# Down product of the experts in rounded parts, on one Trainium2 core

## What is computed

```python
xb = x[token_buf].reshape(E, CAP, H)
gu = jnp.einsum('ech,ehf->ecf', xb, W_gate_up)
g, u = jnp.split(gu, 2, axis=-1)
inter = jax.nn.silu(g) * u
yb = jnp.einsum('eci,eih->ech', inter, W_down)
yb = yb * w_buf.reshape(E, CAP, 1)
routed = jnp.zeros((T, H), x.dtype).at[token_buf].add(yb.reshape(E * CAP, H))
shared = jax.nn.silu(x @ Wsg) * (x @ Wsu) @ Wsd
```

## Time and profile before

| | |
|---|---|
| median of 3 runs | 711.11 us (708.4 to 711.25) |
| profiled execution | 710.25 us, its span 708.6 us |
| PE busy | 675.0 us, 95% of the span |
| PEld busy | 630.5 us, 89% |
| DVE busy | 471.5 us, 67% |
| ACT busy | 331.9 us, 47% |
| POOL busy | 210.5 us, 30% |
| PE's part of the chain that ended last | 67% |

### The profile page before, as it was taken

How to read it: one execution, slowest core, us unless ns; L and a number is a source line. 1 busy time by engine, 2 the same in 40 slices (tenths; PEclk the granted TensorE clock), 3 DMA queues, 4 the chain that set the end, 5 groups by cost and what they waited for, 6 DMA issues and landing times.

```text
span 708.6 us, 16559 instructions
## 1 busy us (share of the span) xinstructions
PE 675.0 (95%) x4587; PEld 630.5 (89%) x4588; DVE 471.5 (67%) x1486; ACT 331.9 (47%) x803; POOL 210.5 (30%) x312
## 2 busy tenths in 40 slices
PE   6979999999999999999999999999999999999993
PEld 6879988999989888889999999999999999999993
DVE  2357788887888888666576666666666666666651
ACT  1335555645556565444444444444444444444431
POOL 3113223232233300310333333333333324242430
PEclk9989999999999999999999999999999999999998
DMA  8136344544444232621454544445464545454531
GB/s 280 44 101 218 112 131 144 172 131 136 145 136 144 88 104 54 181 71 25 99 110 99 110 99 102 108 99 111 97 113 97 113 97 113 97 113 97 113 56 20
DMA packets 74180, 79.36 MB, mean 112 GB/s; under 512 B 6361, under 2 KB 65897, under 8 KB 74154
## 3 DMA queue, kind: packets, MB, share of 16 engines
q1 hardware_dynamic: 61706, 65.81, 33.1%
q0 software_dynamic: 12160, 12.60, 11.0%
q10 hardware_dynamic: 288, 0.66, 0.3%
HBM read 51.73 MB, written 19.32 MB: 100 GB/s over the span
## 4 chain that ended last, share of the span: by engine, by line
PE 67%; DVE 12%; DMA 8%; issue 7%; ACT 2%; POOL 1%; DVEq 1%; POOLq 0%; ACTq 0%; SPq 0%
PE bank L1220 19%; PE bank L1030 9%; PE bank L1190 9%; PE bank L1239 7%; PE bank L1018 6%; PE bank L1202 6%; DMA result<-y_rows,put_idx 5%; PE bank L1060 3%; PE bank L1240 3%; DMA result<-s_rows 1%; DVE s_inter L1657 1%; DVE stats L1387 1%; PE bank L1088 1%; DVE w_raw L1483 1%; DVE h L1411 1%
## 5 line engine op out<-in xcount | busy, mean ns | idle before, releaser
L1657 DVE TENSOR_TENSOR s_inter<-s_gate,bank 128x384 f32<-128x384 f32 (+1 forms) x112 | 60.3, 539 | 68.7 <-PE bank L1220 58.8
L1239 PE MATMUL bank<-s_dn,s_in_hi 128*128 128x384 f32 (+1 forms) x287 | 87.3, 365 | 3.3 <-DVE s_rows L1672 3.0
L865 ACT ACTIVATE s_gate<-bank 128x384 f32<-128x384 f32 (+1 forms) x112 | 53.5, 479 | 67.7 <-PE bank L1220 67.7
L1030 PE MATMUL bank<-w_tok,patches 128*128 128x192 f32 x384 | 72.7, 343 | 8.2 <-DMA patches<-xp 6.9
L689 POOL DMA_INDIRECT result<-y_rows,put_idx x40 | 65.4, 1635 | 38.1 <-DVE y_rows L1644 15.3
L1220 PE MATMUL bank<-all_hiA,s_hi 128*128 (+4 forms) x210 | 73.5, 350 | 2.0 <-DVE s_inter L1657 0.6
L760 ACT ACTIVATE y<-h,shift,rstd 128x192 f32<-128x192 f32 (+2 forms) x96 | 45.6, 538 | 59.4 <-POOL shift L623 59.4
L1030 PEld LDWEIGHTS bank<-w_tok,patches 128*128 128x128 f32 x384 | 65.7, 200 | 8.1 <-issue 8.1
L1240 PE MATMUL bank<-s_dn,s_in_lo 128*128 128x192 f32 (+1 forms) x287 | 72.0, 251 | 0.0
L1220 PE MATMUL bank<-all_B,s_lo 128*128 (+4 forms) x210 | 70.1, 334 | 0.0
L1220 PE MATMUL bank<-all_B,s_hi 128*128 (+4 forms) x210 | 70.1, 334 | 0.0
(11 more groups left out here) (205 smaller groups left out, 1846.4 us busy)
## 6 DMA issues: line engine op xcount, KB each, us to landing
raw_gu<-wgu SPq DMA_DIRECT2D x22, 464.0 KB, 5.0
raw_gu<-wgu SPq DMA_DIRECT2D x44, 232.0 KB, 5.9
patches<-xp SPq DMA_DIRECT2D x16, 588.0 KB, 4.4
down_w<-wdn SPq DMA_DIRECT2D x22, 348.0 KB
result<-s_rows POOLq DMA_DIRECT2D x13, 288.0 KB
result<-h SPq DMA_DIRECT2D x16, 192.0 KB
yw_rows<-y SPq DMA_DIRECT2D x16, 192.0 KB
all_hiA<-y_hiA SPq DMA_DIRECT2D x16, 162.5 KB, 2.6
```

The lines of the kernel that those rows point to most:

```text
L865: act.activation(s_gate[m % 2][0:r, 0:width], up_banks(m, alone)[0][0:r, 0:width], ACT.Silu).then_inc(s_gate_ready, 1)
L1030: mm = pe.matmul(tok_ps[:, t * D:(t + 1) * D], own[:, c, t * 128:(t + 1) * 128], w_tok[:, c, :], start=c == 0, stop=c == KC - 1)
L1239: pe.matmul(bank[0:r, 0:2 * D], s_in_hi[:, m, rows], s_dn[:, m, :], start=m == 0, stop=False)
L1657: dve.tensor_tensor(s_inter[m % 2][0:r, 0:width], s_gate[m % 2][0:r, 0:width], up, ALU.mult).then_inc(s_inter_ready, 1)
```

## The change

The down product is split as the others are. ACT rounds `down_w` to `down_hi` (`down_part`, 116 x 768 in one instruction) and `inter` to `inter_hi` (`inter_part`, two instructions of 116 x 384 for an expert); DVE makes the rests (`down_low`, `inter_low`). `down` then runs three rounded products where one fp32 product stood, so twelve for a half.

The rests need room. `gu_lo` now lies over `raw_gu`, `down_lo` over `down_w` and `inter_lo` over `inter`: each rest is written over the data it is taken from. So the next gate and up weights may be loaded only when the products with `gu_lo` have run, and SP's wait goes from `gu_split` to `gu_mm`. PE's `down` waits for `down_split` and `inter_split` where it waited for the load and for `inter_ready`.

```diff
+        inter_at = chunks.at
...
+        raw_gu_at = experts.at
         raw_gu = [sb(f"raw_gu{p}", [128, 2, 2 * I]) for p in range(2)]
+        down_at = experts.at
         down_w = [sb(f"down_w{p}", [F, EM, D]) for p in range(2)]
...
-        gu_lo = [sb(f"gu_lo{p}", [128, 2, 2 * I], F32R) for p in range(2)]
+        down_hi = [sb(f"down_hi{p}", [F, EM, D], F32R) for p in range(2)]
+        inter_hi = sb("inter_hi", [F, EM, CAP], F32R)
+        over_raw = Region(raw_gu_at).place
+        gu_lo = [over_raw(f"gu_lo{p}", [128, 2, 2 * I], F32R) for p in range(2)]
+        over_down = Region(down_at).place
+        down_lo = [over_down(f"down_lo{p}", [F, EM, D], F32R) for p in range(2)]
+        inter_lo = Region(inter_at).place("inter_lo", [F, EM, CAP], F32R)
...
-                        wait_apart(sp, passed, (gu_split, 4 * j + 2 * n - 2))
+                        wait_apart(sp, passed, (gu_mm, 8 * j + 4 * n - 4))
...
+                def down_part(j, n):
+                    act.wait_ge(down_in[n % 2], arrivals(j, n, n % 2, 16))
+                    act.activation(down_hi[n % 2][:, :, :], down_w[n % 2][:, :, :], ACT.Copy).then_inc(down_hi_ready, 1)
+
+                def inter_part(j, n, i):
+                    act.wait_ge(inter_ready, 8 * j + 4 * n + 2 * i + 2)
+                    own = slice(2 * i, 2 * i + 2)
+                    act.activation(inter_hi[:, own, :], inter[:, own, :], ACT.Copy).then_inc(inter_hi_ready, 1)
...
                 gu_part(0, 0, 1)
+                down_part(0, 0)
...
                     s_hi_part(o, WIDTH, 0)
                     silu(j, 0, 2)
                     s_silu(o, WIDTH, 2)
+                    inter_part(j, 0, 0)
                     s_hi_part(o, WIDTH, 1)
                     gu_part(j, 1, 1)
                     silu(j, 0, 3)
                     s_silu(o, WIDTH, 3)
+                    inter_part(j, 0, 1)
                     s_hi_part(o, WIDTH, 2)
                     split_x(j, 1)
                     s_silu(o, WIDTH, 4)
                     s_hi_part(o, WIDTH, 3)
+                    down_part(j, 1)
                     silu(j, 1, 0)
                     s_hi_part(o, WIDTH, 4)
                     s_silu(o, WIDTH, 5)
...
                     s_hi_part(o, WIDTH, 5)
                     silu(j, 1, 2)
                     s_silu(o, WIDTH, 7)
+                    inter_part(j, 1, 0)
                     s_hi_part(o, WIDTH, 6)
                     s_hi_part(o, WIDTH, 7)
                     silu(j, 1, 3)
                     s_half(o, PER_PAIR * j + ADDED_AHEAD, WIDTH, TILES, 0)
                     split_x(j, 2)
+                    inter_part(j, 1, 1)
                     gu_part(j, 2, 1)
+                    down_part(j, 2)
                     s_half(o, 0, WIDTH, TILES, 1)
                     s_half(o, 0, WIDTH, TILES, 2)
 
...
                         pe.wait_ge(y_ready, 2 * j + n + 1)
-                        pe.wait_ge(down_in[n % 2], arrivals(j, n, n % 2, 16))
-                        pe.wait_ge(inter_ready, 8 * j + 4 * n + 4)
+                        pe.wait_ge(down_split, 2 * j + n + 1)
+                        pe.wait_ge(inter_split, 4 * j + 2 * n + 2)
                     rows = slice(h * CH, (h + 1) * CH)
+                    ps = dn_ps[0:CH, h * D:(h + 1) * D]
+                    w_hi, w_lo = down_hi[n % 2], down_lo[n % 2]
                     for m in range(EM):
-                        mm = pe.matmul(dn_ps[0:CH, h * D:(h + 1) * D], inter[:, m, rows], down_w[n % 2][:, m, :],
-                                       start=m == 0, stop=m == EM - 1)
+                        pe.matmul(ps, inter_hi[:, m, rows], w_hi[:, m, :], start=m == 0, stop=False)
+                        pe.matmul(ps, inter_hi[:, m, rows], w_lo[:, m, :], start=False, stop=False)
+                        mm = pe.matmul(ps, inter_lo[:, m, rows], w_hi[:, m, :], start=False, stop=m == EM - 1)
                     if h == 1:
                         mm.then_inc(dn_mm, 1)
...
+                def down_low(j, n):
+                    dve.wait_ge(down_hi_ready, 2 * j + n + 1)
+                    dve.tensor_tensor(down_lo[n % 2][:, :, :], down_w[n % 2][:, :, :], down_hi[n % 2][:, :, :].bitcast(F32),
+                                      ALU.subtract).then_inc(down_split, 1)
+
+                def inter_low(j, n, i):
+                    dve.wait_ge(inter_hi_ready, 4 * j + 2 * n + i + 1)
+                    own = slice(2 * i, 2 * i + 2)
+                    dve.tensor_tensor(inter_lo[:, own, :], inter[:, own, :], inter_hi[:, own, :].bitcast(F32),
+                                      ALU.subtract).then_inc(inter_split, 1)
+
...
                 gu_low(0, 0, 1)
+                down_low(0, 0)
...
                     s_lo_part(o, WIDTH, 0)
                     gated(j, 0, 2)
                     s_mul(o, WIDTH, 2)
+                    inter_low(j, 0, 0)
                     s_lo_part(o, WIDTH, 1)
                     gu_low(j, 1, 1)
                     gated(j, 0, 3)
                     s_mul(o, WIDTH, 3)
+                    inter_low(j, 0, 1)
                     s_lo_part(o, WIDTH, 2)
                     split_x(j, 1)
                     slots(j, 3, 0)
...
                     slot_weights(j, 1)
                     slots(j, 3, 1)
                     slot_tokens(j, 3)
+                    down_low(j, 1)
                     slot_images(j, 4)
                     weigh(j, 0)
                     gated(j, 1, 0)
...
                     s_lo_part(o, WIDTH, 5)
                     gated(j, 1, 2)
                     s_mul(o, WIDTH, 7)
+                    inter_low(j, 1, 0)
                     s_lo_part(o, WIDTH, 6)
                     s_lo_part(o, WIDTH, 7)
                     gated(j, 1, 3)
                     s_sum(o, WIDTH, TILES, 0)
                     split_x(j, 2)
+                    inter_low(j, 1, 1)
                     slots(j, 4, 0)
                     s_sum(o, WIDTH, TILES, 1)
                     gu_low(j, 2, 1)
                     slot_weights(j, 2)
                     slots(j, 4, 1)
                     slot_tokens(j, 4)
+                    down_low(j, 2)
                     s_sum(o, WIDTH, TILES, 2)
                     weigh(j, 1)
```

4 lines of the change are left out of this document (added).

## The result

The changed kernel takes 706.25 us (median of 5 runs, 704.83 to 708.26), beside 710.6 us for the kernel before on the same chip. The ratio is 0.9946 with a 95% interval of 0.9921 to 0.9971. In a later set of runs it came to 0.9923 (0.9911 to 0.9935). Forecast were 706.8 us against 711.11.

The account below looks back on a forecast made before the run. The loop over expert pairs was taken as a PE stream. Per pair -0.50 + 0.57 for the first expert and -0.50 for the second gave -0.43, ten pairs -4.3: 710.25 - 4.3 + 0.86 = 706.8 us, range 700.5 to 712.5.

Parts of the forecast that it names:

- The products' pace: PE's twelve rounded down products per half follow each other every 0.088 us.
- The rival at 0.101: New down products on PE follow every 0.101 us: about -1 us in all, 710; chance 0.15.
- The gross gain: PE's down products get 0.25 us shorter per half, 0.50 per expert, 1.00 per pair, 10.0 us in all.
- The first place: DVE before L1657 of chunk 3: a 0.47 us step fits 0.46 us idle, cost nothing, hardly a margin.
- The second place: DVE between slot numbers and L1657 of chunk 5: 0.87 us step loses the first expert's 0.50 and 0.07 more.
- The second expert under cover: Second expert's subtractions fall among DVE's waits of 1.41 and 1.04 us, so its 0.50 us gain stays.
- The weights' load: Next gate and up weights, issued about 365.5, land 7.8 us later; ACT waits a little, at no cost.
- The slower rival: Gate and up weights land late, beyond 8.9 us, everything from the rounding 1.2 us late per pair: 718.8; chance 0.14.
- Ahead of the loop: One pair of 768-column instructions under the chunk computed alone: 0 to 0.7 us in all, taken as 0.
- Full gain: DVE's 0.87 us at chunk 5 is hidden as its run closes up: -1.00 a pair, 701.1; chance 0.12.
- The second waiting place: L1657 of chunk 3 also late by its whole step, 0.4 us a pair on top: 710.8; chance 0.17.
- the late weights: Gate and up load's third landing lengthens by 1.2 us over 8.9, ten pairs 12 us: 718.8; chance 0.14.

Follow-up runs that it names:

- The run with both moves: Changed kernel with the first expert's down-weight rounding later and the second expert's 768-column subtraction behind the multiplication of chunk 6: 701.8 us, ratio 0.9883.
- The one with the products alone: Changed kernel without the added VectorE subtractions, its three products all of rounded parts, ScalarE's copies kept: 703.37 us, ratio 0.9864.
- the dose: Changed kernel with one more 384-column VectorE subtraction per pair ahead of gated(j, 0, 3) and the multiplication of chunk 3: 711.35 us, ratio 0.9975.
- the second execution: The changed kernel itself, unaltered, run and profiled once more in set 3: 707.66 us, ratio 0.9923.
- the two variants of the kernel before: Kernel before with only the load's later wait (713.15 us, ratio 1.0001), and with a 384-column subtraction added behind slot_tokens(j, 3) (714.94 us, 1.0024).
- the two runs with the first expert's rounding later: Changed kernel with the very first expert's down-weight rounding and rest later: alone 705.28 us (0.9941); with the 768-column subtraction also moved 701.8 us (0.9883).
- the kernel with one line moved: Changed kernel with the second expert's 768-column subtraction, down_low(j, 1), moved behind the multiplication of chunk 6: 704.63 us, ratio 0.9876.
- The same 0.47 us step: 384-column subtraction added behind down_low(j, 1) in the changed kernel: 711.13 us (1.0011); same place with down_low(j, 1) moved behind chunk 6: 702.61 us (0.9897).

## Why the prediction was right

**The products' pace: held.** 0.088 was taken from the value product with 69 stationary columns, 0.089 was measured with 96. The rival at 0.101 is out. The estimate by the Trainium skill (TensorE: Matmul & The Clock Gate, section LDWEIGHTS), 80 ns from 96 columns at 1.2 GHz, would have given 0.080 and a gross gain near 13 us. With 69 stationary columns the distance was 0.088 and with 96 it is 0.089, so it doesn't go down in proportion to them here, and the trace decides for 0.089.

**The gross gain: held, some 10% too large.** Lined up instruction by instruction with the kernel before, TensorE gains 0.23 and 0.21 us in the two halves of each expert. That is 0.44 an expert and 0.88 a pair, where the prediction had 0.50 and 1.00. The run with both moves gives the 0.88 as it is. The one with the products alone gives it too when it is lined up, and its 1.04 holds the shorter stop at shared product 1.

**The first place: held.** TensorE's product 4 is no later, and the dose showed that there is next to no room (0.09 us).

**The second place: the mechanism held, its size was too large, and something else made it up.** The prediction let L1657 of chunk 5 eat 0.57 us. It was 0.33 in the undisturbed pairs. The first term that failed is the start of VectorE's run, which was to be 0.15 sooner. Its first instruction, the slot numbers (L1601, now L1633), waits for the counting product behind TensorE's first half. In all ten pairs of the kernel before and of the second execution it starts 0.04 us behind the end of that product's record (369.37 + 0.33 = 369.70 and 369.74 before, 369.14 + 0.33 = 369.47 and 369.52 after). So it comes sooner by the whole of what that half has become shorter, and the prediction, which had the half at 0.25, should have taken that. Counted from shared product 4, which starts at 366.13 before and at 366.14 in the second execution, the start went from 3.61 (369.74) to 3.38 (369.52), 0.23 sooner. The other 0.14 closed up inside the run, 0.10 of it at one spot: the subtraction starts 0.08 behind the start of `slot_tok`, where the next instruction had started 0.18 behind it. The multiplication then starts at 7.83 where the prediction had 8.05. The release was 0.15 behind the end instead of 0.13.

By these sizes a pair is -0.44 + 0.33 - 0.44 = -0.55, which is what the second execution gives, against 36.25 and also lined up with the kernel before. The first had -0.38, for the idle time ahead of w_slot cost it about 0.16 a pair more. So the first median of 706.25 fits the sum of -4.3 us partly because two errors and one disturbance that the prediction didn't know offset each other. The second ratio, 0.9923 or 5.4 us, is the one of the corrected sum.

**The second expert under cover: held.** Its gain is full, in the changed kernel and with the other subtraction moved next to it.

**The weights' load: right in result, wrong in size.** Expected were a landing of 7.8 us and a wait of some tenths. It was 5.3 in one execution and 6.4 in the other, and ScalarE didn't wait in either. The slower rival, which needed more than 8.9, went the wrong way: the landing became shorter.

**Ahead of the loop: 0 held.** Up to the first x_hiA it is 40.36 to 40.39 us in all runs but one, and that one was the granted clock. From there to shared product 4 of the first pair it is 29.80 us in the kernel before, and 29.67 and 30.40 in the changed kernel. Of the last, 0.56 are a stop of TensorE with VectorE late behind the landing of the count rows, which the two variants of the kernel before show too (1.05 and 0.77). Without such stops the two runs with the first expert's rounding later take 30.03 and 30.05 there, the other variants with the copies and subtractions 29.8 to 29.9, so that move cost some 0.2 us rather than saving 0.7.

**The rivals.** Full gain was wrong for the change as written, and right for the kernel with one line moved: 0.9876 is 702.3 us on the scale of 711.11, beside the rival's 701.1. Its argument, that VectorE's run would close up, was true for 0.14 us of 0.87. The second waiting place didn't come, and the late weights neither.

## What to carry to other kernels

Where one engine is the stream, count an added instruction on another engine against the idle time of that engine ahead of the next release, place by place. The same 0.47 us step cost 4.6 us in ten pairs where there was none left, and 1.2 where a neighbour had been moved away. If such a step overflows, look first for a place behind the next release: one moved line gave 3.3 or 5.0 us here, by which measurement of the changed kernel it stands beside, where the change itself had brought 5.4 or 3.8. When two executions are compared, line up the whole queue of the engine that is the stream, since a pair's length alone mixes what the change does with stops that the change has no part in. And a stretch in which the feeding engine has no slack also hands on each hiccup of that engine, so a margin of some tenths is worth keeping.
